# Last phase of an attention and mixture-of-experts kernel: work moved from TensorE and VectorE to GpSimd and ScalarE, and the two norms spread over three groups

## The reference

```
def _layernorm(x, axis=-1, eps=1e-05):              # no gain, no bias
    return (x - mean(x)) / sqrt(var(x) + eps)

x = _layernorm(x + attention(x))                    # called x1 in the kernel
gates = softmax(x @ gate_w); top 2 of 8, made to sum to 1 -> combine
y   = each chosen expert's output for each token
out = sum over the two experts of combine * y       # 256 channels per token
out = (out + x - mean) * rsqrt(var + eps) * ln_g + ln_b     # moments of out + x
x   = _layernorm(x + out)                           # the kernel's output
```

## Time and profile before

| what | value |
|---|---|
| median of 3 runs (lowest, highest) | 2387.07 us (2384.43, 2387.57) |
| the profiled execution: time | 2383.96 us |
| its span from first to last instruction | 2382.2 us |
| mean granted clock of TensorE | 0.922 |
| busy in the span | TensorE 89%, VectorE 72%, ScalarE 57%, GpSimd 54% |
| start of the last phase | 2222.19 us |

### The profile page before, as it was taken

The page is one execution under the profiler, slowest core; times in us unless marked ns, Lnnn a source line. Parts: engine busy times, 40 slices in busy tenths (PEclk is TensorE's granted clock), DMA queues, the critical chain, the costliest instruction groups (busy, mean ns, idle before and its releaser), DMA issues. The chain is left out here.

```text
span 2382.2 us, 43666 instructions
## 1 busy us (share of the span) xinstructions
PE 2119.7 (89%) x12268; PEld 1476.8 (62%) x12268; DVE 1715.5 (72%) x5003; ACT 1366.8 (57%) x3316; POOL 1296.8 (54%) x1472
## 2 busy tenths in 40 slices
PE   3898998999899999899899989974399999999598
PEld 2654655565555556465566555533299989988487
DVE  3675687687577677668668767815588888888498
ACT  1265655555555565565565555653278778778254
POOL 2455465655754763666556475551677777776000
PEclk7798999999899898899899899985699999999799
DMA  6555556556555555554655555615022222222575
GB/s 181 123 137 129 113 114 160 116 113 156 116 118 147 121 122 123 133 121 108 163 111 126 143 119 115 135 24 199 23 75 75 75 73 75 75 73 66 165 245 169
DMA packets 190519, 284.47 MB, mean 119 GB/s; under 512 B 54072, under 2 KB 111056, under 8 KB 190160
## 3 DMA queue, kind: packets, MB, share of 16 engines
q1 hardware_dynamic: 168720, 236.43, 41.7%
q0 software_dynamic: 17152, 35.81, 5.0%
q10 hardware_dynamic: 4416, 9.44, 1.1%
HBM read 99.48 MB, written 37.90 MB: 58 GB/s over the span
## 5 line engine op out<-in xcount | busy, mean ns | idle before, releaser
L546 ACT ACTIVATE probs<-scores_T 128x512 f32<-128x512 f32 (+3 forms) x1536 | 654.7, 492 | 256.4 <-PE scores_T L435 253.0
L785 POOL TENSOR_SCALAR_AFFINE_SELECT probs<-probs 128x256 f32<-128x256 f32 x512 | 205.7, 410 | 540.1 <-ACT probs L546 537.4
L494 PE MATMUL ring<-k_stack,q_stack_b 96*128 96x512 f32 (+3 forms) x1024 | 400.7, 434 | 19.9 <-DVE neg_part L693 9.5
L693 DVE TENSOR_REDUCE neg_part<-ring 128x1 f32<-128x512 f32 x512 | 333.5, 684 | 97.5 <-PE ring L494 95.4
L435 PE MATMUL scores_T<-q_stack_b,k_stack 98*128 98x512 f32 (+3 forms) x1024 | 325.9, 396 | 43.8 <-ACT probs L546 42.7
L452 PE MATMUL o_ps<-probs,v_ones 128*17 128x512 f32 (+3 forms) x3072 | 349.6, 529 | 1.4 <-POOL probs L785 1.1
L494 PEld LDWEIGHTS ring<-k_stack,q_stack_b 96*128 96x128 f32 x1024 | 195.4, 200 | 228.4 <-issue 75.1
L698 DVE CUSTOM_DVE_ANT_0 ring<-ring,mask 128x384 f32<-128x384 f32 (+3 forms) x512 | 243.6, 507 | 120.4 <-PE ring L494 118.1
L698 DVE CUSTOM_DVE_ANT_0 ring<-ring,mask,neg_part 128x384 f32<-128x384 f32 (+3 forms) x512 | 260.5, 554 | 74.2 <-PE ring L494 73.4
L1099 ACT ACTIVATE o_sb<-ht_ps,ln_b,ln_g 128x128 f32<-128x128 f32 x544 | 217.9, 450 | 89.4 <-PE ht_ps L1048 89.0
L435 PEld LDWEIGHTS scores_T<-q_stack_b,k_stack 98*128 98x128 f32 x1024 | 192.0, 204 | 101.5 <-ACT probs L546 78.2
(11 more groups left out here) (191 smaller groups left out, 4617.1 us busy)
## 6 DMA issues: line engine op xcount, KB each, us to landing
u_rot<-u SPq DMA_DIRECT2D x128, 256.0 KB, 3.8
k_stack<-u_rot SPq DMA_DIRECT2D x128, 256.0 KB, 4.2
lat_w<-lat_split SPq DMA_DIRECT2D x32, 512.0 KB, 5.9
q_stack_a<-u_rot SPq DMA_DIRECT2D x64, 256.0 KB
q_stack_b<-u_rot SPq DMA_DIRECT2D x64, 256.0 KB
k_stack<-u SPq DMA_DIRECT2D x64, 256.0 KB, 4.3
y<-y_rows SPq DMA_DIRECT2D x32, 512.0 KB, 6.4
x_raw<-in_xT SPq DMA_DIRECT2D x16, 512.0 KB, 6.1
```

Source lines behind the costliest of these rows:

```text
L494: nc.tensor.matmul(out[:, 0:k1 - k0], q_stack[qb // 4][0:3 * L, row_buf(n, qb // 4), h, P * (qb % 4):P * (qb % 4) + P], k_stack[0:3 * L, n ...
L546: nc.scalar.activation(probs[:, s % 2, h, cols], sc[(t + j) % 3][:, HALF - w:HALF], ACT.Exp).then_inc(exp_done, 1)
L693: nc.vector.tensor_reduce(neg_part[:, n % 2, part_col], src[:], AX_X, ALU.max, negate=True).then_inc(max_taken, 1)
L785: nc.gpsimd.affine_select(both, both, [[0, 2], [1, P]], ALU.is_ge, zero, base=0, channel_multiplier=-1).then_inc(kept, 1)
```

## The change

Residual plus bias goes from TensorE to GpSimd, one addition of 128 x 1024 elements per group, from x1 and the bias in SBUF; xb becomes an SBUF tile with two buffers and leaves PSUM, and `row0` goes. The two reciprocal roots go to GpSimd: add epsilon, then raise to the power -0.5. ScalarE's square roots and VectorE's inversions with their correction go. The result of L1281 is multiplied by the reciprocal root on ScalarE, in four instructions, in place, and GpSimd adds xb to it, one addition of 128 x 1024. VectorE takes the moments of that result for group n - 1 while it works on group n, and the shift for group n - 2. ScalarE writes the output of group n - 2 in turn n, after the scalings of n. v gets a third buffer. SyncE's list keeps its order.

```diff
-        row0 = sb("row0", [P, P])
+        xb = [sb(f"xb_{a}", [P, CG, C]) for a in range(2)]
-        v = [sb(f"v_{a}", [P, CG, C]) for a in range(2)]
+        v = [sb(f"v_{a}", [P, CG, C]) for a in range(3)]
...
@@ sync
-                        sp.wait_ge(xb_ready, CG * (n - 2))
+                        sp.wait_ge(xb_ready, n - 2)
...
+        @block.gpsimd
+        def _(pool):
+            def root(i, n):
+                pool.wait_ge(mv_done[i], CG * n + CG)
+                nc.gpsimd.tensor_scalar(ve[:, i, :], mv[:, i, n % 2, :, 1], EPS, None, ALU.add).then_inc(ve_done[i], 1)
+                pool.wait_ge(ve_done[i], n + 1)
+                if i == 1 and n >= 2:
+                    pool.wait_ge(out_ready, CG * (n - 1))
+                nc.gpsimd.tensor_tensor(rstd[:, i, n % 2, :], ve[:, i, :], half[:], ALU.pow).then_inc(rstd_done[i], 1)
+
+            def residual(n):
+                pool.wait_ge(x1_loaded[n % 3], 16 * (n // 3 + 1))
+                if n >= 2:
+                    pool.wait_ge(v_done, n - 1)
+                nc.gpsimd.tensor_tensor(xb[n % 2][:], x1[n % 3][:], b_rep[:].unsqueeze(1).to_broadcast([P, CG, C]),
+                                        ALU.add).then_inc(xb_ready, 1)
+
+            nc.gpsimd.memset(half[:], -0.5).then_inc(half_set, 1)
+            pool.wait_ge(half_set, 1)
+            pool.wait_ge(gb_loaded, 32)
+            residual(0)
+            for n in range(n_groups + 1):
+                if n < n_groups:
+                    root(0, n)
+                    if n + 1 < n_groups:
+                        residual(n + 1)
+                    pool.wait_ge(turned, CG * n + CG)
+                    pool.wait_ge(xb_ready, n + 1)
+                    nc.gpsimd.tensor_tensor(v[n % 3][:], v[n % 3][:], xb[n % 2][:], ALU.add).then_inc(v_done, 1)
+                if n >= 1:
+                    root(1, n - 1)
...
@@ tensor
-                if n >= 1:
-                    pe.wait_ge(v_done, CG * n)
-                for t in range(CG):
-                    nc.tensor.matmul(xb(t), routes["ident"][:], x1[n % 3][:, t, :], start=True, stop=False)
-                    nc.tensor.matmul(xb(t), row0[:], b_rep[:], start=False, stop=True).then_inc(xb_ready, 1)
...
@@ vector
-                nc.vector.tensor_scalar(ve[:, i, :], mv[:, i, d, :, 1], EPS, None, ALU.add).then_inc(ve_done[i], 1)
-            def invert(i, n):
...
+            def scale(n):
+                if n >= 3:
+                    dve.wait_ge(out_ready, CG * (n - 2))
+                for t in range(CG):
+                    nc.vector.scalar_tensor_tensor(out=v[n % 3][:, t, :], in0=f(n, t), scalar=mv[:, 0, n % 2, t, 0:1],
+                                                   in1=g_rep[:], op0=ALU.subtract, op1=ALU.mult).then_inc(scaled, 1)
+
+            def shift(n):
+                d = n % 2
                 dve.wait_ge(rstd_done[1], n + 1)
                 nc.vector.scalar_tensor_tensor(out=nmr[:, d, :], in0=mv[:, 1, d, :, 0], scalar=-1.0,
                                                in1=rstd[:, 1, d, :], op0=ALU.mult, op1=ALU.mult).then_inc(nmr_done, 1)
-            for n in range(n_groups + 1):
+            for n in range(n_groups + 2):
                 if n < n_groups:
                     if n >= 2:
-                        dve.wait_ge(v_done, CG * (n - 1))
-                        dve.wait_ge(sd_done[0], n)
+                        dve.wait_ge(turned, CG * (n - 1))
                     first(n)
-                if n >= 1:
-                    third(n - 1)
+                if n >= 2:
+                    shift(n - 2)
                 if n < n_groups:
-                    invert(0, n)
-                    if n >= 2:
-                        dve.wait_ge(out_ready, CG * (n - 1))
-                    second(n)
+                    scale(n)
+                if 1 <= n <= n_groups:
+                    moments(1, n - 1, lambda t: v[(n - 1) % 3][:, t, :], v_done)
@@ scalar
-            for n in range(n_groups + 1):
+            for n in range(n_groups + 2):
                 if n + 1 < n_groups:
                     diagonals(n + 1)
                 if n < n_groups:
-                    if n >= 1:
-                        act.wait_ge(rstd_done[0], n)
-                    root(0, n)
-                if n >= 1:
-                    m, d = n - 1, (n - 1) % 2
+                    act.wait_ge(rstd_done[0], n + 1)
+                    for t in range(CG):
+                        act.wait_ge(scaled, CG * n + t + 1)
+                        nc.scalar.activation(v[n % 3][:, t, :], v[n % 3][:, t, :], ACT.Identity,
+                                             scale=rstd[:, 0, n % 2, t:t + 1]).then_inc(turned, 1)
+                if n >= 2:
+                    m, d = n - 2, n % 2
                     act.wait_ge(nmr_done, m + 1)
                     if m >= 2:
                         act.wait_ge(stored[d], 16 * (m // 2))
                     for t in range(CG):
-                        nc.scalar.activation(o[d][:, t, :], v[d][:, t, :], ACT.Identity,
+                        nc.scalar.activation(o[d][:, t, :], v[m % 3][:, t, :], ACT.Identity,
                                              bias=nmr[:, d, t:t + 1], scale=rstd[:, 1, d, t:t + 1]).then_inc(out_ready, 1)
-                if n < n_groups:
-                    root(1, n)
```

More of the change, by code:

```diff
@@ L1180, in combine_phase @@
         ve = sb("c_ve", [P, 2, CG])
-        sd = sb("c_sd", [P, 2, CG])
-        guess, err = sb("c_guess", [P, 2, CG]), sb("c_err", [P, 2, CG])
+        half = sb("c_half", [P, CG])
         rstd = sb("c_rstd", [P, 2, 2, CG])
@@ L1186, in combine_phase @@
                 for a in range(3)]
-        xb_ps = [ctx.enter_context(nc.psum_tensor(f"xb_ps{i}", [P, HALF], F32)) for i in range(CG // 2)]
-        xb = lambda t: xb_ps[t // 2][:, C * (t % 2):C * (t % 2) + C]
         f = lambda n, t: f_ps[n % 3][t // 2][:, C * (t % 2):C * (t % 2) + C]
         gb_loaded, diag_ready = sem("gb_loaded"), sem("diag_ready")
-        row0_set = sem("row0_set")
+        half_set, turned = sem("c_half_set"), sem("c_turned")
         x1_loaded = [sem(f"x1_loaded{a}") for a in range(3)]
@@ L1197, in combine_phase @@
         ve_done = [sem("c_ve_done0"), sem("c_ve_done1")]
-        sd_done = [sem("c_sd_done0"), sem("c_sd_done1")]
-        guessed = [sem("c_guessed0"), sem("c_guessed1")]
         rstd_done = [sem("c_rstd_done0"), sem("c_rstd_done1")]
@@ L1239, in _ @@
                     last.then_inc(mixed, 1)
-                if n == 0:
-                    pe.wait_ge(gb_loaded, 32)
-                    pe.wait_ge(row0_set, 2)
-                if n >= 1:
-                    pe.wait_ge(v_done, CG * n)
-                for t in range(CG):
-                    nc.tensor.matmul(xb(t), routes["ident"][:], x1[n % 3][:, t, :], start=True, stop=False)
-                    nc.tensor.matmul(xb(t), row0[:], b_rep[:], start=False, stop=True).then_inc(xb_ready, 1)
         @block.vector
@@ L1256, in moments @@
                 for t in range(CG):
-                    dve.wait_ge(signal, CG * n + (t + 1, t // 2 * 2 + 2)[i == 0])
+                    dve.wait_ge(signal, n + 1 if i else CG * n + t // 2 * 2 + 2)
                     nc.vector.bn_stats(stats[:, i, t, :], src(t)).then_inc(stats_done[i], 1)
@@ L1278, in second @@
-            def second(n):
-                d = n % 2
[L1280 to L1290, removed]
@@ L1292, in third @@
-            def third(n):
-                d = n % 2
-                invert(1, n)
+            def scale(n):
[5 more added lines that the diff above has]
+            def shift(n):
+                d = n % 2
@@ L1297, in third @@
                                                in1=rstd[:, 1, d, :], op0=ALU.mult, op1=ALU.mult).then_inc(nmr_done, 1)
-            nc.vector.memset(row0[:], 0.0).then_inc(row0_set, 1)
-            dve.wait_ge(row0_set, 1)
-            nc.vector.memset(row0[0:1, :], 1.0).then_inc(row0_set, 1)
             dve.wait_ge(gb_loaded, 32)
-            for n in range(n_groups + 1):
+            for n in range(n_groups + 2):
                 if n < n_groups:
                     if n >= 2:
-                        dve.wait_ge(v_done, CG * (n - 1))
-                        dve.wait_ge(sd_done[0], n)
+                        dve.wait_ge(turned, CG * (n - 1))
                     first(n)
-                if n >= 1:
-                    third(n - 1)
+                if n >= 2:
+                    shift(n - 2)
                 if n < n_groups:
-                    invert(0, n)
-                    if n >= 2:
-                        dve.wait_ge(out_ready, CG * (n - 1))
-                    second(n)
+                    scale(n)
+                if 1 <= n <= n_groups:
+                    moments(1, n - 1, lambda t: v[(n - 1) % 3][:, t, :], v_done)
         @block.scalar
         def _(act):
-            def root(i, n):
-                act.wait_ge(ve_done[i], n + 1)
-                nc.scalar.activation(sd[:, i, :], ve[:, i, :], ACT.Sqrt).then_inc(sd_done[i], 1)
```

## The result

The changed kernel takes 2419.14 us (median of 4 runs, 2410.90 to 2420.74) against 2387.32: a ratio of 1.0135, 95% interval 1.0096 to 1.0174. It is slower, by 32 us; forecast were 2416 us and slower. Run again at the end of the study (`after_again`), the ratio was 1.0130, 1.0084 to 1.0176. Ratios go by the fast executions alone, and leave out the few that the chip's second, slower state lengthened; the profile of `late_diag3` is one of these, and `late_diag3_again` repeats it with a fast one.

A forecast was written before the change was run, and what follows sets the result against it. TensorE's 8.63 us per group bounded the last phase; afterwards a two-group loop of 8.3 + 7.6 + 1.1 + 1.5 + 2.2 + 2.0 = 22.7 us per pair adds 30.9 us, giving 2416 us, range 2398 to 2434.

The forecast's parts named there:

- The step that decides: Last phase: output n - 2's store releases loads n + 2, so a 22.7 us loop spans two groups, not three.
- pairs: Groups in the last phase come two together, one pair every 22.7 us, 11.35 per group; chance 0.68.
- The start: First output store of the last phase at 2259.4 instead of 2251.14, loads of group 4 going out 8.3 us late.
- Landing: From the end of an output, through store and loads, to TensorE's start: 8.3 us.
- The cold sum: TensorE's sum after an idle gap, begun at the low clock: 7.6 us, bounds 5.2 and 10.3.
- clock kept: Rival: TensorE stays at 2.4 GHz over gaps, 2.4 us less for each of six sums, 2402 us; chance 0.12.
- low to the end: Rival: low clock through the whole sum after a gap, 2.7 us more on six sums, 2432 us; chance 0.08.
- Moments, root, scalings and output: Loop's steps after the sum: moments 1.1, GpSimd's root 1.5, ScalarE's scalings 2.2, output 2.0 us.
- GpSimd's turn: GpSimd's work per group, two additions and two roots: 7.9 us, bounds 6.6 and 9.3.
- SyncE's wait: SyncE's waiting for ScalarE in the last phase: over 120 us, against 100.7 before.
- The wait of the residual for x: GpSimd's residual addition waiting for x: costed at nothing; uncovered, some 2 us per pair.
- The exclusion: VectorE's two-SBUF-input shift waiting for GpSimd: costed at nothing, 0 to 6 us possible; as general rival 2444 us, chance 0.03.

The follow-up runs named there:

- store_late: The changed kernel with SyncE's store of group n - 4, not n - 3, issued behind the loads of group n: phase 154.0 us, ratio 0.9971 to the kernel before.
- late_diag3: store_late with three buffers of diagonals, made two groups ahead: phase 144.0 us, ratio 0.9951 to the kernel before; repeated, 144.1 us and 0.9957.
- warm: The changed kernel with unused filler products on TensorE behind sums 3 to 14: phase 182.7 us, ratio 1.0084 to the kernel before.
- residual_only: The kernel before with only residual plus bias moved to GpSimd, VectorE reading xb from SBUF: phase 167.2 us, ratio 1.0052 to the kernel before.
- residual_tt: residual_only with VectorE adding epsilon from an SBUF tile by a tensor_tensor with two SBUF inputs: phase 168.3 us, ratio 1.0035 to the kernel before.
- late_split: late_diag3 with each group's fourth-tile sum on VectorE and a third buffer for xb: phase 146.3 us, ratio 0.9935 to the kernel before.
- late_eps: late_diag3 with epsilon added by VectorE from a PSUM tile instead of by GpSimd: phase 138.6 us, ratio 0.9918 to the kernel before.
- before_soon: The kernel before with SyncE's store of group n - 2, not n - 3, behind the loads of n: phase 173.2 us, ratio 1.0035.

## Why the prediction was right

- The step that decides, that the output one turn later and SyncE's unchanged list leave two groups for a loop of 22.7 us, was right: pairs of 22.8 us, and `store_late` takes the loss away by that list alone.
- The start: first store expected 37.2 us into the phase, measured 36.0. Pairs were to be 7.9 and 14.8 us apart, and were 7.27 and 15.6 on average.
- Landing, 8.3 us: too small. Over the six pairs it was 8.8 on average, 8.65 (at 2296.27) to 9.1 (group 4, 2263.80 to 2272.92).
- The cold sum, 7.6: 7.8 on average, 7.0 to 8.5 us to the last moments, depending on when the clock rose. The rivals "clock kept" and "low to the end" are out; `warm` measures 5.4 us for such a sum at the full clock.
- Moments, root, scalings and output, together 6.8: 6.2. Root 1.5 and scalings 2.2 were both too large, 1.35 and 1.7 (the power of 128x4 took 1.03, by the straight line 1.10). So the pair is 8.8 + 7.8 + 6.2 = 22.8, where 8.3 + 7.6 + 6.8 = 22.7 was forecast: errors of +0.5, +0.2 and -0.6. That the 31.1 measured lies beside the 30.9 of the sum is partly luck.
- GpSimd's turn, 7.9, was 7.28. It was to be busy 125 us in the phase, and was 114. SyncE's wait, over 120, was 135.2.
- The wait of the residual for x, costed at nothing: it occurs, 2.0 and 2.18 us in the two pairs around 2300 us, and costs nothing, because GpSimd then waits 5.35 and 6.24 us for VectorE's variances.
- The exclusion, costed at nothing: right for this kernel. The shift, L1295, took 0.16 or 0.17 us all 16 times. It met neither a large addition nor a power; in 14 cases it overlapped the addition of epsilon, 0.22 us on GpSimd, by 0.1 us. The other 4-element operations that would collide went to GpSimd with the roots.
- But the reason that I gave was misread. The spread of 0.47 us in the earlier trace rows is no sign against exclusion. `residual_only`, `residual_tt` and `late_split` show it in full, and the trace of the kernel before had it already, in the row of the other engine (L684 has two SBUF inputs and a median of 0.689 us):

```profile
414.87 2.36 POOL L791 TENSOR_TENSOR y_T<-y_T,inv_rep 128x1024 f32<-128x1024 f32 x1 [0.22 <-DMA inv_rep<-inv_sums]
...
415.34 2.43 DVE L684 TENSOR_TENSOR u<-u,u_rot 128x512 fp32r<-128x512 f32 x1 [4.82 <-ACT u_rot L565]
```

  GpSimd came first and kept its 2.36; VectorE paid. At 606.51, where VectorE's started first (606.42, 0.69 us), GpSimd's took the 2.82 of the spread. By the Trainium skill, page "SBUF — State Buffer", section "Who interferes with whom", the exclusion comes with two SBUF inputs or a fast mode of tensor_scalar. All three runs, the rows above and the PSUM forms agree; the short overlaps of the shift show no wait, and don't decide anything.
- What I missed: the loop over the diagonals, which kept even the mended list of `store_late` from GpSimd's pace.

## What to carry to other kernels

When an output moves a turn later, look for the in-order list that holds its store, and count how many groups the loop from load to load still spans; divide its length by that number and compare with the busiest engine. Where a trace names one releaser for a wait on several, take the named one out before believing it. Before work goes to GpSimd, check which VectorE instructions beside it have two SBUF inputs or are small tensor_scalars on SBUF, look in the trace at hand for the longest time of such an instruction and not only at its median, and give those a PSUM operand.

## What the runs showed of the hardware

- A VectorE instruction of 0.17 us took 0.89 when it met a GpSimd addition of 2.35, and ended with it; so did one with two SBUF inputs of 128x4 (0.88), and one of 128x256 took 2.36. With an operand or the output in PSUM they took 0.16 and 0.17. Moments of an SBUF tile (four in 1.40 us) aren't held up.
- TensorE's clock fell to 1.2 GHz in each gap of over 9 us. It rose 3.3, 5.1 and 6 us into the sums at 2296.27, 2318.38 and 2272.92. After some gaps of 2 to 3 us it fell inside the next sum: 2.03 us in `late_split`, 2.18 in `warm`, 2.55 in `late_eps`; after 2.68 us at 2298.41 in `late_eps` it stayed. In `before_soon`, gaps of up to 1.8 us left it at 2.4 GHz.
- The power of 128x4 on GpSimd takes 1.03 us, against 0.675 for 128x1 and 1.672 for 128x8; on ScalarE four scalings of 128x256 from SBUF take 1.7 us in a row, four outputs with a bias 2.06.
